# Three edits around the fusion of a convolution block: who requests border, weights and parameters, where the filter kernels and the mixing matrices are computed, and what is left in the last stage before the spectral one

## The chip, the cores and the metric

The kernel runs on 1 core of one Trainium2 chip. The metric is the device time of one execution in microseconds (us). The core has TensorE (PE; its weight loads are PEld), VectorE (DVE), ScalarE (ACT), GpSimd (POOL) and SyncE (SP), which meet only at semaphores. DMAs are requested by SP, ACT or POOL, each in the order of its own program, and are carried out by the core's 16 DMA engines. SBUF is the on-chip memory, PSUM the matmul accumulators, "the DRAM tensors" (table, xn, y_dram, kern_dram, spec_dram, t_dram) are in device memory.

## What is computed

The input is x of shape (2, 128, 64, 64), float32. One block adds a convolution part, then a token-mixing part:

```python
# four branches (kernel 1, 1, 3, 7): offsets and mask by a convolution, bilinear samples, contraction
offset = conv2d(x, off_w, off_b, pad); mask = 2 * sigmoid(conv2d(x, mod_w, mod_b, pad))
sampled = bilinear_sample(x, py, px) * mask                      # x, zero outside the image
y = einsum('bckhw,ock->bohw', sampled, reg_w)
x1..x4 = relu(group_norm(y));  x5 = relu(group_norm(conv2d(mean(x), pool_w)))
out = relu(group_norm(conv2d(concat(x1..x5), fuse_w)))           # "the fusion"

# token mixing on u = layernorm(tokens), over four lengths T, T/2, T/4, T/8 with weights w_i
U_plus, U_minus = FFT convolutions of u with 16 filters phi
out_i = sum_k sigma_k**0.25 * (U_plus @ Mpp[i,k] + U_minus @ Mpm[i,k]) + sum_{lag<3} u_shifted @ Mu[i,lag]
w = one_hot(argmax(s)) - s + s,  s = softmax(log_weights + gumbel)
t = t + sum_i w_i * out_i
```

Of this, three products depend on weights alone: the transforms of the filters phi (kern), the matrices mixed over the four lengths and split in a rounded and a rest part (mh, ml, from M_phi, w and sigma), and the same for the lag matrices (mus, from Mu and w).

## The kernel before

The program is a row of stages with a barrier between any two; within a stage each engine has its own list. The times of the stages in the profiled execution are in the next section.

**stage_normalise** (L61) normalises image 0 over its channels in 8 groups of 512 pixels. ACT loads x (L215). For a group PE turns it (L158), DVE measures and scales it (L185 to L203), PE turns it back (L168) and ACT copies it into xnpad (L229). The result is written four times, shifted by a row or a column, into the table that is sampled later: four requests for each half of a group (L113), the first half by SP, the second by ACT; SP also writes xn (L144). The table has a zero border: 16 small writes of the tile zero (L131, L134), which SP requests ahead of everything else in its list, after that the 4410 KB of wom, the weights of the offset convolution (L137), and only then the table and xn. POOL copies seven shifted windows (L122). After the turn of group 4, PE waits for wom and convolves the first window (L253, 49 taps) before it turns groups 5, 6 and 7. The stage ends when all engines are through, SP last of all with its waits for every write.

**stage_branches** (L260) does everything of the branches. ACT first requests base, the bias (into P) and rowt (L521 to L524); DVE waits for all three (`params`) before its first operation, base + P (L606); only after this come the offsets of tile 0, 1, 2, 3 (L615 to L643), each of which lets PE convolve the next window (L253) and POOL gather the samples of the tile (L501). From then on, 960 steps (16 groups of 512 pixels, 60 taps) follow: POOL requests four gathers, DVE and ACT blend the corners (L537, L663 to L674), PE turns and contracts them (L776, L788).

**stage_fuse** (L855) first works out the group norm. Then 16 groups follow in loops of four (`Fori`). SP loads 2048 KB of y_dram into one of four buffers yin as soon as the group four before it is fused (L923). ACT applies scale, bias and relu in place, 8 operations (L976). PE multiplies the 8 pieces with fw (L948; an f32 matmul is two records in the trace, so a group has 16). ACT copies the sum out (L969: `fu`), DVE measures it (L1019). At the end of each four ACT waits for the group's own sum before it goes on with the next four.

**stage_sum** adds x, **stage_tokens** (L1087) normalises the tokens, keeps them in uT and writes their transforms to spec_dram.

**stage_mixtures** (L1270) loads the weights of the token part: taps_dft and windows (phi), the parameters lw, gb, sigma, mu, and m_phi in four chunks of 2048 KB (mr). DVE and ACT work out the weights w_i (`wi`) and sigma**0.25. PE transforms the filters in 8 pieces (L1443), ACT rounds each (L1358), DVE takes the rest (L1402), SP stores the three parts to kern_dram. For each of 4 chunks DVE mixes m_phi (L1421 to L1427), ACT rounds (L1363), DVE takes the rest (L1432). Among this PE computes the lag products: 16 regions with 12 matmuls each (24 records, L1453) into two accumulators ps_m, which DVE adds to accum (L1412), four regions after each chunk; SP stores accum to t_dram.

**stage_spectral** and **stage_output** follow and are not touched.

Of the kernel before, what the change touches and what calls it, by code (L numbers as in the profile page):

```python
# [5 lines left out]
B, C, H, W = 2, 128, 64, 64  # L6
HW = H * W
# [6 lines left out]
TS = H + 3  # L14
# [12 lines left out]
S = 16  # L27
# [39 lines left out]
def stage_normalise(nc, x, tables, ident, eps6, xpart, xn, w_om, wom, R, ps_shared):  # L67

    ctx = ExitStack()
    with ctx:  # L70
# [17 lines left out]
        border_written = sem("border_written")  # L88
# [26 lines left out]
        @block.gpsimd  # L115
        def _(pool):
            pool.memset(zero[:], 0.0).then_inc(zero_set, 1)
            pool.memset(xnpad[:], 0.0).then_inc(pad_zeroed, 1)
            pool.wait_ge(pad_zeroed, 1)
            pool.wait_ge(xn_copied, 2)  # L120
            for kx in range(7):
                pool.tensor_copy(first_win[:, kx, :, :], xnpad[:, 0:HR, kx:kx + W]).then_inc(first_copied, 1)  # L122
            pool.wait_ge(first_copied, 7)

        @block.sync
        def _(sp):
            sp.wait_ge(zero_set, 1)
            for slot, (dy, dx) in enumerate(((0, 0), (0, 1), (1, 0), (1, 1))):
                part = slice(slot * C, (slot + 1) * C)
                for y0, y1 in ((0, 2 - dy), (TS - 1 - dy, TS)):  # L130
                    sp.dma_start(grid[y0:y1, :, part].rearrange("y x s -> x y s"),  # L131
                                 zero[:, 0:(y1 - y0) * C].rearrange("p (y s) -> p y s", s=C)).then_inc(border_written, 16)
                for x0, x1 in ((0, 2 - dx), (TS - 1 - dx, TS)):
                    sp.dma_start(grid[2 - dy:TS - 1 - dy, x0:x1, part],  # L134
                                 zero[0:TS - 3, 0:(x1 - x0) * C].rearrange("p (x s) -> p x s", s=C))\
                        .then_inc(border_written, 16)
            sp.dma_start(wom[:], w_om).then_inc(wom_loaded, 16)  # L137
# [9 lines left out]
            sp.wait_ge(border_written, 256)  # L147
# [3 lines left out]
        def _(pe):  # L151
# [11 lines left out]
            for i in range(GI):  # L163
# [70 lines left out]
        with nc.Block() as clearing:  # L234
            @clearing.sync
            def _(sp):
                for s in x_loaded + [zero_set, border_written, pad_zeroed, x_turned, var_ready, sd_ready,
# [22 lines left out]
def stage_branches(nc, x, xn, tables, wom, R, ps_shared, base_om, bias_om, row_off, regw, ident, eps6, om_dram, y_dram, ystats, xpart):  # L260

    ctx = ExitStack()
    with ctx:
# [4 lines left out]
        base = sb("base", [128, 3, TAPS])  # L268
        rowt = sb("rowt", [128, NG * 4])
# [3 lines left out]
        P = sb("P", [128, 3, TAPS])  # L273
# [34 lines left out]
        params = sem("om_params")  # L308
# [211 lines left out]
        def _(act):  # L520
            act.dma_start(base[:], base_om).then_inc(params, 16)  # L521
            act.dma_start(P[:], bias_om.rearrange("(a k) t -> a k t", a=1).to_broadcast([128, 3, TAPS]))\
                .then_inc(params, 16)
            act.dma_start(rowt[:], row_off).then_inc(params, 16)  # L524
# [76 lines left out]
        def _(dve):  # L601
# [3 lines left out]
            dve.wait_ge(params, 48)  # L605
# [249 lines left out]
def stage_fuse(nc, gate, y_dram, ystats, xpart, pool_w, fuse_w, gnp, gnf, blk16, blk8, eps5, fu, fa, fb):  # L855

    ctx = ExitStack()
    with ctx:
# [27 lines left out]
        fsd = sb("fsd", [C, B])  # L886
        ps_s = ctx.enter_context(nc.psum_tensor("ps_s", [128, 2, 64], F32))
# [21 lines left out]
        fsd_ready = sem("fsd_ready")  # L909
# [955 lines left out]
```

## Time and profile before

| | us |
|---|---|
| Runs (3): median, lowest, highest | 6398.62, 6391.32, 6402.8 |
| Profiled execution: its own time | 6402.89 |
| Its span, first to last instruction | 6401.2 |
| stage_normalise | 0 to 87 |
| stage_branches | 87 to 4955 |
| stage_fuse | 4956 to 5121 |
| stage_sum, stage_tokens | 5121 to 5239 |
| stage_mixtures | 5239 to 5342 |
| stage_spectral, stage_output | 5342 to 6401 |

Over the span PE is busy 82%, DVE 76%, POOL 61%, ACT 41%. These are averages over stages with different limits. The profile is read by stages: in each, which engine's list or which transfer ends last. Its own time is 1.7 us more than its span. A row of a timeline gives the start in us, the time it covers in us, the engine (SPq and ACTq are requests of DMAs by SP and ACT), the line, the operation, what it writes and reads, how many instructions (x), and in brackets how long the engine was idle before it and what ended that.

### The profile page before, as it was taken

The numbers are of one execution on the slowest core, as the hardware profiler recorded it, in microseconds if no ns is written. First come the engines' busy times: TensorE is split into PE (matmuls) and PEld (weight loads), VectorE is DVE, ScalarE is ACT, GpSimd is POOL, SyncE is SP. The second block draws the span as 40 slices with busy tenths as digits, with TensorE's granted clock in tenths as the row PEclk, the third lists the DMA queues.
The fourth block names the chain that finished last, engine by engine and source line by source line (L and its number), as shares of the span: only waits on it lengthen the run. The fifth ranks groups of instructions, "written<-read, shape, count | busy, mean of one in ns | idle before, by whom it ended". The sixth has DMA issues, their size and how long they took to land. (4 is left out here: it accounts for less than half of the span.)

```text
span 6401.2 us, 66500 instructions
## 1 busy us (share of the span) xinstructions
PE 5219.2 (82%) x16608; PEld 2633.4 (41%) x16608; DVE 4849.9 (76%) x6696; ACT 2640.8 (41%) x6416; POOL 3908.6 (61%) x4370
## 2 busy tenths in 40 slices
PE   4988888788887878888887888876666748999998
PEld 4433333333333333333333333322222326777777
DVE  2888988888788888878788887878777165666664
ACT  0343434343333434333333333333333633666663
POOL 2777777777777777777777777777776002222221
PEclk8999999999999999999999989998887878999999
DMA  6787877777777777777777777777776565555555
GB/s 219 217 243 223 243 230 243 230 223 221 227 228 219 226 224 222 222 226 218 228 216 234 210 233 210 231 212 229 220 213 202 208 236 183 148 148 146 152 152 178
DMA packets 582036, 1359.17 MB, mean 212 GB/s; under 512 B 95452, under 2 KB 262784, under 8 KB 579972
## 3 DMA queue, kind: packets, MB, share of 16 engines
q0 software_dynamic: 327680, 1044.66, 55.9%
q1 hardware_dynamic: 225748, 292.33, 14.2%
q10 hardware_dynamic: 28336, 19.10, 1.0%
q8 instruction: 104, 1.70, 0.1%
q14 instruction: 168, 1.38, 0.1%
HBM read 1240.28 MB, written 115.46 MB: 212 GB/s over the span
## 5 line engine op out<-in xcount | busy, mean ns | idle before, releaser
L501 POOL DMA_INDIRECT G<-table,om x3840 | 3633.4, 946 | 1215.2 <-issue 1154.0
L788 PE MATMUL ps_y<-sT,R 128*128 128x512 f32 x3840 | 2028.1, 656 | 24.0 <-ACT yb L553 23.8
L663 DVE TENSOR_TENSOR G<-G,ps_w 128x1536 f32<-128x1536 f32 x960 | 1681.4, 1751 | 468.2 <-DMA G<-table,om 452.4
L537 ACT ACTIVATE ps_a<-G,om 128x128 f32<-128x128 f32 x3840 | 1192.6, 357 | 1812.8 <-DMA G<-table,om 1130.6
L776 PE MATMUL ps_t<-ident,acc 128*128 128x128 f32 x3840 | 662.2, 298 | 909.1 <-DVE acc L674 890.4
L776 PEld LDWEIGHTS ps_t<-ident,acc 128*128 128x128 f32 x3840 | 433.6, 147 | 1665.9 <-DVE acc L674 1554.6
L545 ACT ACTIVATE sT<-ps_t 128x512 f32<-128x512 f32 x960 | 572.2, 596 | 1109.0 <-PE ps_y L788 1106.7
L788 PEld LDWEIGHTS ps_y<-sT,R 128*128 128x128 f32 x3840 | 722.5, 209 | 593.3 <-issue 590.7
L1580 DVE TENSOR_TENSOR vl<-ps_v,vh 128x512 fp32r<-128x512 f32 x1024 | 656.9, 686 | 335.0 <-ACT vh L1529 335.0
L1514 POOL DMA_DIRECT2D ut<-spec_dram x512 | 262.6, 513 | 895.8 <-PE ps_v L1595 637.8
L667 DVE TENSOR_TENSOR ps_a<-G,ps_a 128x512 f32<-128x512 f32 x960 | 668.5, 696 | 131.0 <-ACT ps_a L537 31.8
L674 DVE TENSOR_TENSOR acc<-G,ps_a 128x512 f32<-128x512 f32 x960 | 659.7, 687 | 103.0 <-DVE ps_a L671 4.1
L758 PE MATMUL ps_c<-xr,wom 128*128 128x512 f32 x1470 | 721.2, 611 | 0.0
L758 PE MATMUL ps_shared<-xr,wom 128*52 128x512 f32 x1470 | 719.4, 609 | 0.0
L1529 ACT ACTIVATE vh<-ps_v 128x512 fp32r<-128x512 f32 x1024 | 580.4, 596 | 297.6 <-PE ps_v L1595 270.9
L671 DVE TENSOR_TENSOR ps_a<-G,ps_a 128x512 f32<-128x512 f32 x960 | 667.1, 695 | 31.8
L758 PEld LDWEIGHTS ps_c<-xr,wom 128*128 128x128 f32 x1470 | 291.8, 200 | 379.7 <-issue 379.7
L1618 PE MATMUL ps_yf<-vh,mh 128*128 128x512 f32 x1024 | 413.6, 404 | 0.0
L1618 PE MATMUL ps_yf<-vh,ml 128*128 128x512 f32 x1024 | 411.2, 402 | 0.0
L1618 PE MATMUL ps_yf<-vl,mh 128*128 128x512 f32 x1024 | 409.2, 400 | 0.0
L1595 PE MATMUL ps_v<-tt,ut 96*128 96x512 f32 x1024 | 367.5, 401 | 16.8 <-DMA ut<-spec_dram 14.9
L758 PEld LDWEIGHTS ps_shared<-xr,wom 128*52 128x52 f32 x1470 | 154.9, 126 | 505.6 <-issue 505.6
(184 smaller groups left out, 2407.6 us busy)
## 6 DMA issues: line engine op xcount, KB each, us to landing
tt<-kern_dram SPq DMA_DIRECT2D x512, 192.0 KB, 3.4
G<-table,om POOLq DMA_INDIRECT x3840, 3.7
y_dram<-yb SPq DMA_DIRECT2D x64, 512.0 KB, 4.7
yin<-y_dram SPq DMA_DIRECT2D x16, 2048.0 KB, 8.3
ut<-spec_dram POOLq DMA_DIRECT2D x256, 96.0 KB, 3.3
spec_dram<-spec_hi SPq DMA_DIRECT2D x64, 256.0 KB, 2.6
ut<-spec_dram POOLq DMA_DIRECT2D x256, 48.0 KB, 3.0
om_dram<-om_next SPq DMA_DIRECT2D x60, 150.0 KB, 3.5
```

Source lines behind the costliest of these rows:

```text
L501: pool.indirect_dma_start(G[k % RING][:, j, :], None, tables[g // GI], bass.IndirectOffsetOnAxis(ap=om[g % 2][:, j, 0, k:k + 1].bitcast(I3 ...
L537: last = nc.scalar.activation(ps_a[:, j, :], G[k % RING][:, j, 0:C], ACT.Copy, scale=om[g % 2][:, j, 1, k:k + 1])
L663: nc.vector.tensor_tensor(three, three, ps_w[:, :, h:h + 1].to_broadcast([128, 12, C]) .rearrange("p (j c) d -> p j c d", j=4), ALU.mult). ...
L667: nc.vector.tensor_tensor(ps_a[:, :, :], corner(1), ps_a[:, :, :], ALU.add).then_inc(added, 1)
L671: nc.vector.tensor_tensor(ps_a[:, :, :], corner(2), ps_a[:, :, :], ALU.add).then_inc(added, 1)
L674: nc.vector.tensor_tensor(acc[n % 3][:, :, :], corner(3), ps_a[:, :, :], ALU.add).then_inc(blended, 1)
L758: last = nc.tensor.matmul(ps_c2 if rest else ps_c[:, :], cols[:, 128:128 + REST] if rest else cols[:, 0:128], rows, start=(tap == 0), stop ...
L776: last = nc.tensor.transpose(ps_t[:, 128 * j:128 * j + 128], acc[n % 3][:, j, :], ident[:, :])
L788: last = nc.tensor.matmul(ps_y[:, half, :], R[:, k, 128 * half:128 * half + 128], sT[n % 2][:, :], start=(k == t0), stop=(k == ends[br] - 1))
L1529: nc.scalar.activation(vh[c][:, n, :, :], spread(ps_v[n % BANKS]), ACT.Copy).then_inc(v_high, 1)
L1580: nc.vector.tensor_tensor(vl[c][:, n, :, :], spread(ps_v[n % BANKS]), vh[c][:, n, :, :].bitcast(F32), ALU.subtract).then_inc(v_low, 1)
L1618: last = nc.tensor.matmul(ps_y[q][:, :], m[:, c, k, :], v[c][:, :, k, :], start=(c == 0 and k == 0 and n == 0), stop=(c == 1 and k == KF - ...
```

## The change

**Start.** The 16 border writes are requested by POOL: the 8 of rows behind its two memsets, the 8 of columns behind its window copies. base, the bias and rowt are requested by SP as its first requests in stage_normalise (their tiles live longer now). wom is requested by ACT behind its 8 loads of x. SP's list begins with these three and goes on with table and xn. PE convolves the first window behind the turns of all eight groups. DVE no longer waits for parameters in stage_branches.

**Fusion.** The loops of four are written out, so that ACT applies relu to group g before it copies out g-1, for all g. Between the groups stands what was in stage_mixtures, apart from the lag products: PE transforms filter piece g-2 behind group g (g = 2 to 9), ACT rounds and DVE subtracts piece g-4, DVE mixes a chunk of m_phi at g = 4, 7, 10, 13, and ACT and DVE split it at g = 6, 9, 12, 15. SP's loads and stores for this stand between its loads of y. mr is one buffer (before: two), kern_hi and kern_lo hold a quarter each of what they held.

**stage_mixtures** holds only the lag products, into four accumulators, the adds and the stores of t_dram.

The core of the diff:

```diff
@@ stage_normalise: POOL, SP, PE, ACT
             pool.wait_ge(pad_zeroed, 1)
+            pool.wait_ge(zero_set, 1)
...
+            for slot in range(4):
+                dy, dx = divmod(slot, 2)
+                zero_rows(slot, 0, 2 - dy)
+                zero_rows(slot, TS - 1 - dy, TS)
             pool.wait_ge(xn_copied, 2)
             for kx in range(7):
                 pool.tensor_copy(first_win[:, kx, :, :], xnpad[:, 0:HR, kx:kx + W]).then_inc(first_copied, 1)
+            for slot in range(4):
+                dy, dx = divmod(slot, 2)
+                zero_columns(slot, dy, 0, 2 - dx)
+                zero_columns(slot, dy, TS - 1 - dx, TS)
             pool.wait_ge(first_copied, 7)
+            pool.wait_ge(border_written, 256)
 
         @block.sync
         def _(sp):
-            sp.wait_ge(zero_set, 1)
-            for slot, (dy, dx) in enumerate(((0, 0), (0, 1), (1, 0), (1, 1))):
...
-            sp.dma_start(wom[:], w_om).then_inc(wom_loaded, 16)
+            sp.dma_start(base[:], base_om).then_inc(params, 16)
+            sp.dma_start(P[:], bias_om.rearrange("(a k) t -> a k t", a=1).to_broadcast([128, 3, TAPS])).then_inc(params, 16)
+            sp.dma_start(rowt[:], row_off).then_inc(params, 16)
...
-                if i == 4:
-                    pe.wait_ge(first_copied, 7)
-                    pe.wait_ge(wom_loaded, 16)
-                    convolve_window(nc, ps_shared, first_win, wom, 0).then_inc(first_done, 1)
+            pe.wait_ge(first_copied, 7)
+            pe.wait_ge(wom_loaded, 16)
+            convolve_window(nc, ps_shared, first_win, wom, 0).then_inc(first_done, 1)
...
                 act.dma_start(xg[i][:, :], x[0, :, i * CH:i * CH + CH]).then_inc(x_loaded[i], 16)
+            act.dma_start(wom[:], w_om).then_inc(wom_loaded, 16)
@@ stage_branches: DVE
             dve.sem_inc(sig_used, 1)
-            dve.wait_ge(params, 48)
@@ stage_fuse
+        mixed_at = {4 + 3 * c: c for c in range(NM)}
+        split_at = {6 + 3 * c: c for c in range(NM)}
...
+            def store_kernel(q):
+                sp.wait_ge(k_low, 2 * q + 2)
...
+            for g in range(YR, NG):
+                load_y(g)
+                if g in (9, 12, 15):
+                    load_m(g // 3 - 2)
+                if g % 2 == 0 and 8 <= g <= 14:
+                    store_kernel(g // 2 - 4)
...
+            def kernel_transform(n):
+                q, c = kernels[n]
+                if n == 0:
+                    pe.wait_ge(phi_loaded, 32)
+                if n >= 2:
+                    pe.wait_ge(k_low, n - 1)
...
+            for g in range(NG):
...
+                last.then_inc(fused, 1)
+                if 2 <= g < 2 + NK:
+                    kernel_transform(g - 2)
...
+                last.then_inc(z_ready, 1)
+                if g:
+                    copy_out(g - 1)
+                if g == 2:
+                    act.wait_ge(z_max_ready, 1)
+                    nc.scalar.activation(ys[:], lw[:], ACT.Exp, bias=sm[:, 1:2]).then_inc(e_ready, 1)
+                    nc.scalar.activation(sg[:], sg[:], ACT.Sqrt).then_inc(sig_rooted, 1)
...
+                if 4 <= g < 4 + NK:
+                    round_kernel(g - 4)
+                if g in split_at:
+                    round_mixed(split_at[g])
+            copy_out(NG - 1)
...
+            for g in range(NG):
+                dve.wait_ge(fu_ready, g + 1 + YR)
+                nc.vector.bn_stats(fstats[:, 6 * g:6 * g + 6], fu[:, g * CH:g * CH + CH]).then_inc(fu_measured, 1)
+                if g == 0:
+                    segment_max()
+                if g == 2:
+                    segment_weights()
+                if 4 <= g < 4 + NK:
+                    split_kernel(g - 4)
+                if g in mixed_at:
+                    mix(mixed_at[g])
+                if g in split_at:
+                    split_mixed(split_at[g])
@@ stage_mixtures
+        ps_m = [ctx.enter_context(nc.psum_tensor(f"ps_m{q}", [C, 4, NB], F32)) for q in range(4)]
...
             for n, (b, p, q) in enumerate(regions):
-                pe.wait_ge(added, n + 1)
+                if n >= 4:
+                    pe.wait_ge(added, n - 3)
```

Two places show how the lists moved. First SP at the head of stage_normalise, before (zero is the border's tile, the branch is the stage's entry, xt a group of image 0):

```order
L125 UNCONDITIONAL_BRANCH
L131 DMA table0<-zero 67x2x128
L131 DMA table0<-zero 67x128
L134 DMA table0<-zero 64x2x128
...
L137 DMA wom<-in_w_om 128x8820
L113 DMA table0<-xt0 64x4x128 x4
L144 DMA xn0<-xnpad 128x770
```

and now:

```order
L146 UNCONDITIONAL_BRANCH
L148 DMA base<-in_base_om 128x180
L149 DMA P<-in_bias_om 128x180
L150 DMA rowt<-in_row_off 128x64
L114 DMA table0<-xt0 64x4x128 x4
L157 DMA xn0<-xnpad 128x770
```

The 16 border writes and wom are gone from the front of SP's list; the table's writes stand behind three small loads.

Second PE in the fusion, with the semaphores that a row waits for. Before, in the loop's body (groups 0 and 1 of the four; a row of REGISTER_ALU counts for the next wait):

```order
L948 MATMUL ps_f0<-yin0,fw 128x512 [waits fu_ready,z_ready]
L948 MATMUL ps_f0<-yin0,fw 128x512 x7
L945 REGISTER_ALU
L948 MATMUL ps_f1<-yin1,fw 128x512 [waits fu_ready,z_ready]
L948 MATMUL ps_f1<-yin1,fw 128x512 x7
```

and now (groups 3 and 4, each followed by a filter piece ps_k):

```order
L1025 MATMUL ps_f3<-yin3,fw 128x512 [waits fu_ready,z_ready]
L1025 MATMUL ps_f3<-yin3,fw 128x512 x7
L1017 MATMUL ps_k1<-windows,taps_dft 128x512
L1025 MATMUL ps_f0<-yin0,fw 128x512 [waits fu_ready,z_ready]
L1025 MATMUL ps_f0<-yin0,fw 128x512 x7
L1017 MATMUL ps_k0<-windows,taps_dft 128x512 [waits k_low]
```

From group 4 to group 9 a filter piece that waits for DVE (`k_low`) stands between two groups on PE. What it waits for is the subtraction in DVE's list, here at group 4, behind the measure of that same group; before, the only DVE row of a group was its measure (L1019):

```order
L1164 BN_STATS fstats<-fu 128x6 [waits fu_ready]
L1142 TENSOR_TENSOR kern_lo<-ps_k,kern_hi 128x512 [waits k_high]
L1149 TENSOR_SCALAR mw<-mr,wi 128x1024 [waits m_loaded]
L1151 SCALAR_TENSOR_TENSOR mw<-mr,wi,mw 128x1024 [waits s_step] x3
L1153 TENSOR_TENSOR mt<-mw 128x512 [waits s_step]
```

The subtraction and the mixing of a chunk have moved from stage_mixtures to behind a measure.

## Rows read from the trace of the kernel before

**Rows 1.** Busy time by stage: us, PE, PEld, DVE, ACT, POOL, granted clock, DMA share, GB/s.
```profile
0.00:87.00 87.00, 30.51 (x162) 26.77 (x162) 26.08 (x112) 7.79 (x17) 10.98 (x15) 0.92 0.72 213
...
4955.00:5121.00 166.00, 124.38 (x268) 54.36 (x268) 20.50 (x65) 103.45 (x147) 0.00 (x0) 0.86 0.59 207
...
5239.00:5342.00 103.00, 72.77 (x400) 59.48 (x400) 50.85 (x87) 14.68 (x29) 0.00 (x0) 0.81 0.51 199
```

**Rows 2.** Timeline of SP's requests in stage_normalise.
```profile
4.59 2.68 SPq L131 DMA_DIRECT2D table<-zero  x2
...
33.95 5.12 SPq L134 DMA_DIRECT2D table<-zero  x2
39.11 0.60 SPq L137 DMA_DIRECT2D wom<-in_w_om  x1
...
76.81 3.97 SPq L113 DMA_DIRECT2D table<-xt  x4
80.82 0.61 SPq L144 DMA_DIRECT2D xn<-xnpad  x1
```

**Rows 3.** Timeline of ACT's requests and of PE in stage_normalise.
```profile
29.42 2.79 ACTq L113 DMA_DIRECT2D table<-xt  x4
...
53.09 15.83 PE L253 MATMUL ps_shared<-wom,R 128*128 128x180 f32 x98 [25.80 <-DMA wom<-in_w_om]
...
73.50 3.65 ACTq L113 DMA_DIRECT2D table<-xt  x4
```

**Rows 4.** The DMA request of wom: count, size, us to landing.
```profile
wom<-in_w_om SPq DMA_DIRECT2D x1, 4410.0 KB, 13.8
```

**Rows 5.** Timeline at the head of stage_branches, DVE and POOL.
```profile
103.23 0.35 DVE L606 TENSOR_TENSOR base<-base,P 128x180 f32<-128x180 f32 x1 [24.36 <-DMA rowt<-in_row_off]
...
108.43 1.16 POOL L501 DMA_INDIRECT G<-table,om  x1 [19.90 <-DVEq L646]
```

**Rows 6.** Costliest groups of the page: the gathers; busy, mean ns, idle before.
```profile
L501 POOL DMA_INDIRECT G<-table,om x3840 | 3633.4, 946 | 1215.2 <-issue 1154.0
```

**Rows 7.** Timeline of the fusion: PE, ACT and DVE at groups 0 to 3.
```profile
4973.77 15.84 PE L948 MATMUL ps_f<-yin,fw 128*128 128x512 f32 x32 [6.65 <-ACT yin L976]
...
4983.41 0.69 ACT L969 ACTIVATE fu<-ps_f,bias 128x512 f32 x1 [4.07 <-PE ps_f L948]
...
4984.00 5.73 ACT L976 ACTIVATE yin<-yin,ybb,ya 128x512 f32<-128x512 f32 x8
...
4984.39 0.69 DVE L1019 BATCH_NORM_STATS2 fstats<-fu  x1 [17.08 <-ACT fu L969]
...
4989.78 14.00 PE L948 MATMUL ps_f<-yin,fw 128*128 128x512 f32 x32 [0.18 <-ACT yin L976]
```

**Rows 8.** Timeline of the fusion: PE from group 4, DVE at the last group.
```profile
5010.51 19.92 PE L948 MATMUL ps_f<-yin,fw 128*128 128x512 f32 x40 [6.72 <-ACT yin L976]
...
5116.57 0.69 DVE L1019 BATCH_NORM_STATS2 fstats<-fu  x1 [6.16 <-ACT fu L969]
```

**Rows 9.** DMA requests of the fusion.
```profile
yin<-y_dram SPq DMA_DIRECT2D x16, 2048.0 KB, 8.3
```

**Rows 10.** DMA requests of stage_mixtures.
```profile
mr<-in_m_phi SPq DMA_DIRECT2D x4, 2048.0 KB, 11.4
```

**Rows 11.** Timeline of stage_mixtures.
```profile
5251.12 1.28 ACT L1352 ACT_TABLE_LOAD   x1 [22.45 <-DVE sm L1374]
...
5261.97 0.69 DVE L1402 TENSOR_TENSOR kern_lo<-ps_k,kern_hi 128x512 fp32r<-128x512 f32 x1 [2.20 <-ACT kern_hi L1358]
...
5267.92 6.77 PE L1453 MATMUL ps_m<-uT,mus 128*128 128x64 f32 x48
...
5270.14 3.92 DVE L1423 SCALAR_TENSOR_TENSOR mw<-mr,wi,mw 128x1024 f32<-128x1024 f32 x3
...
5285.23 1.67 DVE L1432 SCALAR_TENSOR_TENSOR ml<-mt,sigma_b,mh 128x256 fp32r<-128x256 f32 x4
...
5336.96 0.69 DVE L1412 TENSOR_TENSOR accum<-accum,ps_m 128x512 f32<-128x512 f32 x1 [2.62 <-PE ps_m L1453]
```

More of the change, by code:

```diff
@@ L64, in first_window, with stage_normalise @@
     return flat(R[:, WIN_TAP:TAPS, :])[:, 0:7 * HR * W].rearrange("c (k r x) -> c k r x", k=7, r=HR)
-def stage_normalise(nc, x, tables, ident, eps6, xpart, xn, w_om, wom, R, ps_shared):
+def stage_normalise(nc, x, tables, ident, eps6, xpart, xn, w_om, wom, R, ps_shared, border_written,
+                    base_om, bias_om, row_off, base, P, rowt):
     ctx = ExitStack()
@@ L257, in convolve_window, with stage_branches @@
     return last
-def stage_branches(nc, x, xn, tables, wom, R, ps_shared, base_om, bias_om, row_off, regw, ident, eps6, om_dram, y_dram, ystats, xpart):
+def stage_branches(nc, x, xn, tables, wom, R, ps_shared, base, P, rowt, regw, ident, eps6, om_dram, y_dram, ystats, xpart):
     ctx = ExitStack()
@@ L886, in stage_fuse @@
         fsd = sb("fsd", [C, B])
+        lw = sb("lw", [128, SEG])
+        gb = sb("gb", [128, SEG])
+        sm = sb("sm", [128, 4])
+        ys = sb("ys", [128, SEG])
+        wi = sb("wi", [128, SEG])
+        sg = sb("sigma_b", [128, KF])
+        mu = sb("mu", [C, SEG, 3, C])
+        mr = sb("mr", [C, KC, 2, SEG, C])
+        mw = sb("mw", [C, KC, 2, C])
+        mt = sb("mt", [C, 2, KC, C])
+        windows = sb("windows", [NB, 2, 2 * S * KF])
+        taps_dft = sb("taps_dft", [NB, 4, NF])
+        khi = [sb(f"kern_hi{h}", [NF, 2, 2 * S * KF], F32R) for h in range(2)]
+        klo = [sb(f"kern_lo{h}", [NF, 2, 2 * S * KF], F32R) for h in range(2)]
+        ps_k = [ctx.enter_context(nc.psum_tensor(f"ps_k{q}", [NF, CH], F32)) for q in range(2)]
         ps_s = ctx.enter_context(nc.psum_tensor("ps_s", [128, 2, 64], F32))
@@ L1014, in _ @@
             nc.vector.tensor_copy(bias5[:], ps_s[:, 1, 0:B]).then_inc(b5_ready, 1)
[L1015 to L1020 removed]
+            ss = Steps(dve, s_step)
@@ L1021, in _ @@
+            dve.wait_ge(m_split, KF)
             dve.wait_ge(fu_measured, NG)
@@ L1434, in _ @@
-            dve.wait_ge(m_split, KF)
+            for n, (b, p, q) in enumerate(regions):
+                dve.wait_ge(mixed, n + 1)
+                acc = accum[:, 2 * b + p, 4 * q:4 * q + 4, :]
+                nc.vector.tensor_tensor(acc, acc, ps_m[n % 4][:, :, :], ALU.add).then_inc(added, 1)
         @block.tensor
         def _(pe):
-            pe.wait_ge(phi_loaded, 32)
-            for n, (q, c) in enumerate(kernels):
-                if n >= 2:
-                    pe.wait_ge(k_low, n - 1)
-                nc.tensor.matmul(ps_k[n % 2][:, :], taps_dft[:, q, :], windows[:, c, :],
-                                 start=True, stop=True).then_inc(k_done, 1)
@@ L1452, in _ @@
                         s0 = 1 + 4 * q + shift
-                        last = nc.tensor.matmul(ps_m[n % 2][:, :, lo:hi], mus[:, lag, seg, :],
+                        last = nc.tensor.matmul(ps_m[n % 4][:, :, lo:hi], mus[:, lag, seg, :],
                                                 uT[:, 2 * b + src, s0:s0 + 4, lo:hi],
@@ L1765, in program @@
             ps_shared = held.enter_context(nc.psum_tensor("ps_shared", [128, CH], F32))
-            stage_normalise(nc, d["x"], tables, ident, eps6, xpart, xn, d["w_om"], wom, R, ps_shared)
-            stage_branches(nc, d["x"], xn, tables, wom, R, ps_shared, d["base_om"], d["bias_om"], d["row_off"], d["regw"], ident, eps6,
+            base = held.enter_context(nc.sbuf_tensor("base", [128, 3, TAPS], F32))
+            P = held.enter_context(nc.sbuf_tensor("P", [128, 3, TAPS], F32))
+            rowt = held.enter_context(nc.sbuf_tensor("rowt", [128, NG * 4], F32))
+            stage_normalise(nc, d["x"], tables, ident, eps6, xpart, xn, d["w_om"], wom, R, ps_shared, border_written,
+                            d["base_om"], d["bias_om"], d["row_off"], base, P, rowt)
+            stage_branches(nc, d["x"], xn, tables, wom, R, ps_shared, base, P, rowt, d["regw"], ident, eps6,
                            om_dram, y_dram, ystats, xpart)
```

344 lines of the change are left out of this document (143 added, 201 removed).

## The prediction, made before the changed kernel had run

> **What bounds the kernel now.** I read the profile by stages, since no engine bounds the whole span. First the page's group of gathers [rows 6]: 3840 gathers of 946 ns, each with some 0.30 us of POOL's own issue before it (1154 us for all), make 4787 us of the 4868 us of stage_branches. That is 5.0 us for each of the 960 steps, and nothing in the change is in these steps. So this stage keeps its length from its first gather on, and what counts is when that gather starts. Three places are left: the time up to the first gather (108.4 us, [rows 5]), the fusion (166 us) and stage_mixtures (103 us, [rows 1]).
>
> Up to the first gather, SP's list is what ends last. Its border writes run from 4.59 to 39.07, wom is requested at 39.11, and the last write of xn at 80.82 [rows 2]; the stage ends at 87.1. PE idled 25.8 us for wom and then convolved for 15.83 us [rows 3]. In the next stage DVE starts at 103.23 only, released by rowt, a small load that lies behind the large loads of that moment [rows 5]: 16.1 us after the stage's start.
>
> In the fusion PE does a group in 7.0 us at full clock (32 records, two groups, in 14.00) and ACT's relu takes 5.73 us [rows 7]. At the end of each four groups PE waits 6.7 us for ACT, and its next groups begin at the lower clock level: 40 records in 19.92 us [rows 8], where 40 at 14.00/32 take 17.5, so 2.4 us more. From PE's first group to the last group's measure it takes 5116.57 - 4973.77 = 142.8 us [rows 7, 8].
>
> In stage_mixtures DVE and the loads set the pace: PE is busy 72.8 us of 103 and DVE 50.9 [rows 1], yet they alternate. The lag products alone are 6.77 us for two regions [rows 11].
>
> **The start.** (a) Parameters. They are requested 80 us earlier, so DVE's wait of 16.1 us goes. What is next: DVE needs only the first window's sum, which PE has finished before the stage begins. R's load is first needed after three windows. Gain 16 us; I see no row that would take it back.
>
> (b) Border and wom. SP loses 34.5 us at the front of its list (4.59 to 39.07). What is late next has three candidates. First, SP's own remaining list: eight groups of four table writes and one of xn, 3.97 + about 0.7 us each when ACT writes too [rows 2], from 14.3 us on: 52, plus about 5 for landing and barrier. Second, the DMA engines. They are busy 0.72 of 87 us [rows 1] = 62.6 us, and none of this work goes. Started at 4.3 and kept at 0.95 it ends at 70; with 2 us of barrier, 72. Third, ACT and then PE. ACT's table writes lie behind wom in its own queue. Alone it needs 3.3 us a group (2.79 of requests and the rest, [rows 3]), with SP beside it 3.65 (the requests, [rows 3]) + 0.9; eight groups from 14.3 are 40 to 51. wom takes 13.8 us to land [rows 4], and a queue that is full of it holds ACT up by at most about 9 us more. Then PE's convolution, 15.8 us [rows 3], now stands behind the last turn instead of the fifth: its end is 40 + 15.8 = 56 at the earliest, about 57 + 15.8 = 73 at the latest likely, and 2 us of barrier. I take 73 for the end of the stage, since the second and the third candidate both point there: 14 us gained. The ends are 57 (30 us gained) and 87 (nothing gained, if writes of 512 bytes from three queues hinder each other).
>
> The Trainium skill, in "DMA: Bandwidth & Descriptors", section "Issuing engines are not separate DMA queues", says that transfers requested by several engines run on the same 16 DMA engines and interleave, so that spreading requests saves only the time of issuing them. This speaks against part (b). By that rule the 62.6 us of work stay a floor and the stage ends at 72; without it, by the lists alone, at 57 to 59.
>
> POOL's 16 border requests: those of rows lie in POOL's idle time before its copies, those of columns behind them. No row shows such a request on POOL; the nearest are gathers at 1.25 us [rows 6], 20 us in all, from about 9 to 45. That is before 73, so I put nothing. Even at SP's 2.2 us each they would be done at 50.
>
> Start: -14 - 16 = -30 us, ends -16 and -46.
>
> **The fusion.** Removed: the stops of the loops. With relu(g+1) issued before copy-out(g), ACT needs 5.73 + 0.69 = 6.4 us a group, under PE's 6.9, so the wait of 6.7 us and the 2.4 us of lower clock after each four are gone. Added on the path:
> - At group 2 ACT loads two tables (1.28 us each [rows 11]) and does three small operations, about 3.5 us. Relu(3) ends that much later; PE waits about 2.0 us and does its first filter piece, 0.9 us (two records of 14.00/32). Together 2.9. The second piece waits for nothing: 0.9.
> - Pieces 2 to 7, behind groups 4 to 9, wait for DVE. After PE ends a group, ACT starts the copy-out 0.15 us later, DVE's measure starts 0.98 us after it (4983.41 to 4984.39 [rows 7]), the subtraction 0.65 later, and it takes 0.74 to release PE (its 0.69 and the step [rows 11]); then the piece, 0.87. That is 3.4 us between two groups, six times: 20.4. I assume that PE keeps its full clock over a wait of 2.5 us.
> - ACT's splitting at groups 6 and 9 hides in these waits. At group 12 ACT has 5.73 + 0.69 + 1.71 = 8.1 us, 1.1 more than PE.
> - DVE's mixing (3.92 for three of its six operations [rows 11], 6.0 in all) lies behind the subtraction at groups 4, 7, 10, 13, in periods of 10.3 or 7 us: hidden.
>
> Sum: groups 0 and 1 16.0, fourteen groups of 6.9 are 96.6, then 2.9 + 0.9 + 20.4 + 1.1, and 1.1 to the last measure: 139.0, against 142.8. Behind the last measure DVE splits the last chunk, 1.67 us [rows 11], which nothing hides. Fusion: -3.8 + 1.7 = -2 us.
>
> The transfers: 34 MB became about 50 MB. y comes in 8.3 us for 2048 KB [rows 9], mr in 11.4 [rows 10]; the loads of y are requested four groups ahead, two are needed at most at once, and through the slow groups each has 20 us. The tight end is the last: y 15 lies behind the last kern stores, which wait for DVE, and the last mr behind y 15. By these rows it lands about where DVE wants it, 3 us late, with 0.4 us to spare for ACT. Each us later costs one. At wom's rate (4410 KB in 13.8 us [rows 4]) all transfers need 152 us instead of the 147 that are there: +5.
> Ends for the fusion: -6 (two of the six waits shorter) and +17.
>
> **stage_mixtures.** 103 us become: eight times 6.77 = 54.2 us of PE [rows 11], with 2.4 us for a start at the lower level [rows 8], the last add 0.69 at 5336.96 and from its end to the stage's end 4.9 us [rows 11], 0.3 at the start: 62.5. With four accumulators DVE's adds are hidden (0.69 against 3.39 a region). Gain 40 us; ends 37 (3.4 us a region become 3.6) and 42.
>
> **The sum.** -30 - 2 - 40 = -72 us. The profiled execution took 6402.9 us (span 6401.2), so it would take 6331. The median of the three runs is 6398.6, 4 us less: 6326.6. I predict 6327.
>
> **The rivals.**
> 1. The fusion grows (17%). The six waits of 2.5 us let PE's clock fall, each paid with 2.4 us [rows 8]: +14. For it: PE's granted clock is 0.86 over the fusion [rows 1]. Against it: the falls shown come behind waits of 6.7 us. 6341.
> 2. The start gives only the parameters' wait (13%): the DMA engines are slower with mixed writes, the stage still ends near 87. For it: 0.72 of busy share already. 6341.
> 3. The start gives all (17%): the stage ends at 57, when SP's and ACT's lists are through. For it: 0.28 of the engines' time is free, and small writes on one queue are slow by their issue. 6311.
> 4. Slower (3%). PE stays at its lower level through the whole fusion, because filter pieces and waits break its work up. Fourteen groups cost 6.9 us more each, the eight pieces 0.9: +104. With the start and stage_mixtures as forecast: 6398.6 - 70 + 102 = 6431. It decides from about two thirds of the groups at the lower level on.
> 5. The change doesn't do what it says (2%): the work moved into the fusion is paid there in full (DVE and the transfers, 40 us) and the start's gain is lost behind the first gathers: within 0.2% of before.
> Forecast as summed: 48%.
>
> **Range and chances.** 6303 to 6350 holds cases 1 to 3 and the forecast with the ends of their terms (-46 - 6 - 42 = -94 is its far edge, taken as 6305 less the runs' spread). A measurement of this kernel can tell about 0.2% (13 us) from no change. Faster by more than that: 95%; within: 2%; slower: 3%.
>
> **What would show it.** Right: the first stage ends near 73 and the first gather starts near 78; DVE's first operation of stage_branches comes within 1 us of its start; the last gather starts as many us earlier as the first. In the fusion PE waits for DVE's subtraction six times, some 2.5 us each, and no longer for ACT at each fourth group; clock 1.0 after the first groups. stage_mixtures about 62 us, PE without gaps. Wrong: a wait of ACT for y or of DVE for mr near the fusion's end; PE records of 0.86 us spacing in the middle of the fusion; ACT held at its table writes behind wom for more than 10 us; or gathers with a period other than 5.0 us.

## The result and the profile after

| | before | changed |
|---|---|---|
| Median of 5 runs each (lowest, highest), us | 6396.09 (6391.32, 6402.8) | 6363.78 (6359.82, 6364.0) |
| Profiled execution, its span | 6402.89, 6401.2 | 6363.91, 6362.2 |
| stage_normalise ends at | 87.1 | 80.2 |
| first gather, last gather start at | 108.4, 4936.2 | 85.7, 4943.2 |
| stage_fuse | 4956.0 to 5121.4 | 4963.6 to 5125.9 |
| stage_mixtures | 5239.3 to 5342.5 | 5244.1 to 5306.2 |
| rest of the span | 1058.7 | 1056.1 |

The ratio is 0.9944 with a 95% interval of 0.9933 to 0.9955: 0.56% faster, 39 us by the spans where 72 were forecast. 6363.8 lies above the range's end of 6350. In spans: first gather -22.7, the stream of gathers +29.7, what lies between it and the fusion +0.6, fusion -3.1, sum and tokens +0.3, mixtures -41.2, the last stages -2.6.

The rows that answer to those shown of before. The page's groups of gathers, as [rows 6] (busy, mean ns, idle before):

```profile
L510 POOL DMA_INDIRECT G<-table,om x3840 | 3660.3, 953 | 1202.2 <-issue 1157.8
```

953 ns instead of 946. POOL's own issue hardly differs (1157.8 us against 1154.0). Of the one line (name, count, ns of the shortest, median and longest, start of first and last), before and then changed:

```profile
L501 POOL DMA_INDIRECT G<-table,om x3840: 942/946/1158, 108.4 to 4936.2; - x192
```

```profile
L510 POOL DMA_INDIRECT G<-table,om x3840: 947/953/1061, 85.7 to 4943.2; - x192
```

The shortest has grown by 5 ns and the median by 7: nearly every gather is some 7 ns longer, from the first hundreds to the last. 3840 x 7 ns are 27 us, POOL's issue adds 3.8 us, and first to last gather takes 4857.5 us instead of 4827.8.

Busy time by stage, as [rows 1], of the changed kernel:

```profile
0.00:80.20 80.20, 30.53 (x162) 26.62 (x162) 26.51 (x112) 7.78 (x17) 26.55 (x31) 1.00 0.85 234
4963.50:5125.90 162.40, 124.36 (x284) 54.35 (x284) 60.18 (x136) 116.77 (x176) 0.00 (x0) 0.92 0.85 312
5244.00:5306.00 62.00, 56.48 (x384) 53.31 (x384) 11.00 (x16) 0.00 (x0) 0.00 (x0) 0.94 0.17 68
```

In the first stage the DMA engines are 0.85 busy for 80.2 us: 68.2 us of work, where before they had 0.72 x 87 = 62.6. Its timeline (ACT's requests, POOL's, SP's, then PE and the next stage, as [rows 2, 3, 5]):

```profile
9.04 0.46 ACTq L228 DMA_DIRECT2D wom<-in_w_om  x1
...
22.34 11.46 ACTq L114 DMA_DIRECT2D table<-xt  x3
33.85 0.61 ACT L242 ACTIVATE xnpad<-ps_n 128x512 f32<-128x512 f32 x1 [15.52 <-issue]
```

```profile
9.06 11.06 POOL L124 DMA_DIRECT2D table<-zero  x8 [0.31 <-POOL xnpad L119]
...
40.69 4.56 POOL L128 DMA_DIRECT2D table<-zero  x8
...
85.69 1.03 POOL L510 DMA_INDIRECT G<-table,om  x1 [4.04 <-DVEq L650]
```

```profile
19.33 14.99 SPq L114 DMA_DIRECT2D table<-xt  x4
...
73.22 0.61 SPq L157 DMA_DIRECT2D xn<-xnpad  x1
```

```profile
63.04 14.46 PE L266 MATMUL ps_shared<-wom,R 128*128 128x180 f32 x98
```

Both queues are held at group 1's table writes (11.5 and 15 us), ACT's copy of group 1 comes at 33.85, PE's convolution at 63.04 and the stage ends at 80.2. POOL's 8 requests of rows take 11.06 us, 1.38 each in the mean, its 8 of columns 0.57 each. Requests of the border (count, KB, us to landing):

```profile
table<-zero POOLq DMA_DIRECT2D x4, 67.0 KB, 17.0
table<-zero POOLq DMA_DIRECT2D x4, 64.0 KB, 3.6
```

Rows (67 KB, requested at 9 us beside wom) land after 17 us, columns (64 KB, requested at 41 us) after 3.6. In the next stage DVE's first operation comes 0.3 us after the stage's start: the wait of 16 us of [rows 5] is gone.

The fusion, PE, as [rows 7, 8] (one group and one filter piece; six of these waits), and its end:

```profile
5014.84 7.03 PE L1025 MATMUL ps_f<-yin,fw 128*128 128x512 f32 x16
5023.96 1.12 PE L1017 MATMUL ps_k<-windows,taps_dft 128*128 128x512 f32 x2 [2.10 <-DVE kern_lo L1142]
```

```profile
5109.59 0.76 DVE L1149 TENSOR_SCALAR mw<-mr,wi 128x1024 f32<-128x1024 f32 x1 [3.20 <-DMA mr<-in_m_phi]
...
5119.43 0.69 DVE L1164 BATCH_NORM_STATS2 fstats<-fu 128x6 f32<-128x512 f32 x1 [3.19 <-ACT fu L1043]
5120.04 1.65 DVE L1159 SCALAR_TENSOR_TENSOR ml<-mt,sigma_b,mh 128x256 fp32r<-128x256 f32 x4
```

stage_mixtures, as [rows 11]:

```profile
5244.10 56.48 PE L1461 MATMUL ps_m<-uT,mus 128*128 128x64 f32 x384 [12.29 <-PEq L1236]
```

The fusion and stage_mixtures came as forecast; the start gave less, and the gathers took back more than the start gave: the last gather starts 7.0 us later than before, though the first starts 22.7 us earlier.

### The profile page after: what moved, and what is told of

Same layout as the page of the kernel before. It is cut to its first block and busy times, and to the rows that moved or that the text cites. A ratio compares the mean times of both kernels' runs of the same rounds, so it can differ in the third digit from the quotient of the medians.

```text
span 6362.2 us, 66252 instructions
## 1 busy us (share of the span) xinstructions
PE 5196.9 (82%) x16608; PEld 2627.8 (41%) x16608; DVE 4850.7 (76%) x6696; ACT 2639.4 (41%) x6416; POOL 3950.9 (62%) x4386
## 3 DMA queue, kind: packets, MB, share of 16 engines
q14 instruction: 168, 1.38, 0.1%
## 5 line engine op out<-in xcount | busy, mean ns | idle before, releaser
L510 POOL DMA_INDIRECT G<-table,om x3840 | 3660.3, 953 | 1202.2 <-issue 1157.8
```

Of the source, the lines that this page charges most:

```text
L510: pool.indirect_dma_start(G[k % RING][:, j, :], None, tables[g // GI], bass.IndirectOffsetOnAxis(ap=om[g % 2][:, j, 0, k:k + 1].bitcast(I3 ...
```

## The experiments

The kernels are named by what they change. "Stream" is the time from the first gather to the last; the page's ns per gather stands beside it.

| kernel | border by | ns | stream, us | first gather | profiled run, us |
|---|---|---|---|---|---|
| before | SP, 16 | 946 | 4827.8 | 108.4 | 6402.9 |
| changed | POOL, 16 | 953 | 4857.5 | 85.7 | 6363.9 |
| border_sp | SP, 16 | 946 | 4829.2 | 96.2 | 6344.5 |
| fusion_alone | SP, 16 | 946 | 4826.1 | 109.1 | 6356.4 |
| border_pool_alone | POOL, 16 | 953 | 4853.4 | 96.7 | 6413.4 |
| merged_on_pool | POOL, 8 | 953 | 4857.5 | 75.1 | 6353.1 |
| border_merged | SP, 8 | 946 | 4830.7 | 88.4 | 6343.0 |
| merged_by_act | ACT, 8 | 946 | 4828.1 | 90.7 | 6341.8 |
| rows_of_64 | POOL, 8 of 64 | 949 | 4841.0 | 74.9 | 6336.1 |

**1. Which edit makes the gathers longer: border_sp, border_pool_alone, fusion_alone.** border_sp is the changed kernel without this:

```diff
-            for slot in range(4):
-                dy, dx = divmod(slot, 2)
-                zero_rows(slot, 0, 2 - dy)
-                zero_rows(slot, TS - 1 - dy, TS)
...
+            for slot, (dy, dx) in enumerate(((0, 0), (0, 1), (1, 0), (1, 1))):   # sync, behind rowt
```

> The changed kernel with one edit undone: SP requests the 16 border writes again (behind the three parameter loads, ahead of the table), POOL requests nothing before its gathers. The semaphore border_written and the held tiles base, P, rowt stay where the change put them. Theory A (POOL's own 16 plain requests make each later gather longer): the gathers are 946 ns again instead of 953, first to last gather 4828 us instead of 4857.5; the start is some 4 us later than in the changed kernel because SP's list begins with 34 us of border writes again; time about 6364 - 29 + 4 = 6339. Theory B (the tiles that live longer, or the semaphore allocated further out, make the gathers longer): still 953 ns and 4857 us, time about 6368.

border_pool_alone makes the opposite edit in the kernel before:

> The kernel before with one edit: the 16 border writes are requested by POOL (rows behind its memsets, columns behind its window copies), with the semaphore border_written allocated outside the stage. wom stays on SP, now its first request; parameters, fusion and mixtures as before. Theory A (POOL's plain requests make the gathers longer): gathers of 953 ns, first to last 4857 us; the stage's end some 7 to 9 us earlier, DVE's wait for rowt stays; time about 6396 + 30 - 8 = 6418, slower than before. Theory B (held tiles): gathers of 946 ns, about 6388.

fusion_alone has the whole start as before (functions stage_normalise and stage_branches):

> The changed kernel with the whole start undone: stage_normalise and stage_branches as before, only the fusion and stage_mixtures are the changed ones. Both theories A and B: gathers of 946 ns, first gather at 108, fusion and mixtures as in the changed kernel (162 and 62 us, -3 and -41, and 2.6 us in the last stages): 6396 - 47 = 6349, faster than the full change. Rival C (the longer program of the fusion makes the gathers longer): gathers of 953 ns, about 6378.

Measured: border_sp 946 ns, median 6345.57, ratio to before 0.9917 (0.9901 to 0.9934). border_pool_alone 953 ns, 6414.09, 1.0023 (1.0013 to 1.0034). fusion_alone 946 ns, 6356.12, 0.9933 (0.9917 to 0.995).

```profile
L501 POOL DMA_INDIRECT G<-table,om x3840 | 3633.4, 946 | 1200.9 <-issue 1156.9
```

```profile
L509 POOL DMA_INDIRECT G<-table,om x3840 | 3660.3, 953 | 1215.1 <-issue 1158.2
```

(border_sp, then border_pool_alone.) Theory A holds: one edit undone gives the 7 ns back and 19 us of the whole; the same edit alone costs 7 ns in the kernel before and makes it slower, although the first gather starts 11.7 us earlier. B and C fall. fusion_alone has 7.5 us less of span than the full change: its first gather is 23.4 us later and its stream 31.4 us shorter. So by the spans the whole edit of the start made the kernel slower; the intervals of the two ratios overlap, so this loss is not clear of noise.

**2. Why the start gave less: wom_behind_3.**

```diff
-            act.dma_start(wom[:], w_om).then_inc(wom_loaded, 16)
...
                 write_table(act, i, 1)
+                if i == 3:
+                    act.dma_start(wom[:], w_om).then_inc(wom_loaded, 16)
```

> The changed kernel with wom requested by ACT behind its table writes of group 3 instead of ahead of all its table writes. Theory D (ACT's table writes held behind wom for 11.5 and 15 us delay the turns, and PE's convolution behind them ends the stage at 80.2): ACT's writes of group 1 take about 3 us, PE's last turn comes near 52 instead of 62, the stage ends at about 70, time about 6354. Rival E (the DMA engines, 0.85 busy over 80 us = 68 us of work, set the end whatever the order): the stage ends at 76 to 80, time 6360 to 6364. The gathers stay 953 ns by theory A and B.

Measured: median 6365.87, 0.9948 (0.9929 to 0.9968), first gather at 85.3 instead of 85.7. One of its four executions took 13926 us and is not in the ratio; the other three took 6362.66 to 6366.46. ACT's hold of 11.5 us in group 1 is gone, but it comes back at group 5, behind the new place of wom, with 12.5 us:

```profile
45.49 7.60 ACTq L114 DMA_DIRECT2D table<-xt  x1
...
53.12 4.87 ACTq L114 DMA_DIRECT2D table<-xt  x3
```

Two stretches of it, with the columns of [rows 1]:

```profile
40.00:50.00 10.00, 2.23 (x8) 1.43 (x8) 5.46 (x20) 1.48 (x4) 1.54 (x3) 0.50 1.02 326
50.00:60.00 10.00, 0.00 (x0) 0.00 (x0) 1.11 (x4) 0.78 (x2) 0.00 (x0) 0.50 1.02 371
```

The DMA engines are full from 40 to 60 while PE does next to nothing. The time is the one that theory E gave, and moving wom within ACT's list doesn't help. Theory D is not refuted by it, since the edit moved ACT's hold instead of taking it away. The other kernels with wom behind ACT's loads of x show how the two hang together. PE's convolution in border_sp and in merged_on_pool (below):

```profile
43.03 15.08 PE L257 MATMUL ps_shared<-wom,R 128*128 128x180 f32 x98
```

```profile
52.58 14.29 PE L257 MATMUL ps_shared<-wom,R 128*128 128x180 f32 x98
```

With no border request on POOL, ACT's three requests at group 1 take 3.5 us and PE's convolution starts at 43.0; with 8 it is 5.8 and 52.6, with 16 it is 11.5 and 63.0. So POOL's border writes beside wom lengthen ACT's hold, and no run here has the one without the other. In border_sp SP's own list, which has the border again, ends the stage at 90.6.

**3. What of the border writes it is: semaphores, requests, pieces, instructions.** border_on_gathered lets the 16 writes signal the semaphore of gather buffer 0, two_semaphores gives the columns a second new one.

> The changed kernel, all 16 border writes still requested by POOL, but they signal a semaphore that the gathers use anyway (that of buffer 0; the waits of buffer 0 count 256 more). border_written is gone. Theory S (each gather costs more because POOL's queue has one semaphore more to serve): 946 ns again, first to last gather 4828 us, 6364 - 29 = 6335. Theory N (the plain requests themselves, their number or their place in POOL's queue): 953 ns, 6364.

> The changed kernel, but the 8 writes of columns signal a second new semaphore. Theory S: the gathers grow once more, to about 960 ns, first to last gather some 4885 us, about 6391. Theory N: 953 ns, 4857 us, 6364.

Both: 953 ns, streams of 4856.5 and 4855.9, 6363.84 and 6360.76 in one run each. The semaphores are not it.

> Kernel border_sp with one of its 16 border writes (top rows of slot 0) requested by POOL on a semaphore of its own, the other 15 by SP. If the 7 ns come with any plain request of POOL ahead of the gathers (or with the one more semaphore that its queue then signals): 953 ns, first to last gather 4857 us, about 6375 for the whole. If they come with the number of requests or descriptors: 946 ns or little more (7/16 ns more), about 6346.

> Kernel one_on_pool with its one POOL request cut into 16 (the same 134 pieces of 512 bytes, 16 requests). Theory R (the number of plain requests ahead of the gathers shifts something by request): gathers of 953 ns as with 16 border writes, first to last gather 4857 us. Theory P (the number of pieces, 134 against some 1570, counts) or theory I (POOL's instructions) with few of them: 946 ns, 4828 to 4830 us.

```diff
-            pool.dma_start(grid[0:2, :, 0:C]...
+            for i in range(16):
+                x0, x1 = 4 * i, 4 * i + 4 if i < 15 else TS
+                pool.dma_start(grid[0:2, x0:x1, 0:C]...
```

> Kernel border_sp and, on POOL, one additional request of 1536 pieces of 4 bytes (from zero into a tile that nothing reads). Theory P: 953 ns, 4857 us. Theory R: 946 ns, 4828 us, as with one request.

> Kernel border_sp with 48 small memsets on POOL behind its window copies, no DMA added. Theory I (the place of POOL's instructions, shifted by the new ones ahead of the gathers, is what counts): 953 ns. Theories R and P: 946 ns, 4828 us.

All four: 946 ns, streams of 4830.0, 4829.8, 4831.0 and 4830.5, 6343 to 6346 us. Neither a request as such, nor 16 of them, nor one with 1536 pieces (of 4 bytes, into SBUF), nor POOL's other instructions lengthen a gather. Theories R, P (in this form) and I fall.

**4. Rows or columns: rows_on_pool, columns_on_pool, merged_early.**

> Kernel border_sp with the 8 writes of rows requested by POOL at 9 us (on a semaphore of its own) and the 8 of columns by SP. Theory L (what counts is that POOL has requests of columns behind its copies): gathers of 946 ns, 4828 to 4830 us from first to last. Theory K (what counts is whether SP's list has border writes at its front, whoever does the rest): 946 ns. Theory P (the number of pieces that POOL has sent ahead of the gathers, some 800 here): 953 ns, 4857 us.

> Kernel border_sp with the 8 writes of columns requested by POOL behind its copies and the 8 of rows by SP. Theory L: 953 ns, 4857 us. Theory K: 946 ns, 4828 us. Theory P (some 770 pieces): 953 ns.

> Kernel merged_on_pool with all 8 writes requested at 9 us, ahead of POOL's window copies. Theory L (late requests): 946 ns, 4830 us, about 6325. Theories K and P: 953 ns, 4857 us, about 6352.

rows_on_pool 953 ns (stream 4855.4), columns_on_pool 946 ns (4830.0), merged_early 953 ns (4857.6). L, K and P all fall: rows on POOL do it, columns don't, with as many requests (8 each) and nearly as many pieces (804 and 768). Their landings differ too:

```profile
table<-zero POOLq DMA_DIRECT2D x4, 67.0 KB, 17.6
```

```profile
table<-zero POOLq DMA_DIRECT2D x4, 64.0 KB, 2.9
```

(rows_on_pool, columns_on_pool.) But this comes from the moment of the request. The rows are requested at 9 us beside wom, the columns at 33 us. Columns requested at 11 us (merged_early) land late as well, and the rows of wom_behind_3, which has no wom beside them, land after 6.6 us:

```profile
table<-zero POOLq DMA_DIRECT2D x2, 128.0 KB, 14.5
```

```profile
table<-zero POOLq DMA_DIRECT2D x4, 67.0 KB, 6.6
```

Yet the gathers of wom_behind_3 take 954 ns. So a slow landing is not the cause. A row has 67 pieces a side, a column 64. Not tried were rows requested late and columns requested early without rows; the moment alone is not it, since one_on_pool and sixteen_small request at 9 us (946 ns) and columns_of_61 (below) at 33 us (949 ns).

**5. 67 against 64: rows_of_64, columns_of_61.** The base of the first is merged_on_pool (below), that of the second columns_on_pool; what POOL leaves out, SP requests.

```diff
-                pool.dma_start(grid[y, :, s0:s1], zero[:, 0:s1 - s0]).then_inc(border_written, 16)
+                pool.dma_start(grid[y, 0:64, s0:s1], zero[0:64, 0:s1 - s0]).then_inc(border_written, 16)
```

> Kernel merged_on_pool, with POOL's four requests of rows covering 64 of the 67 pieces of a row; SP requests the last three pieces of each (four requests at the front of its list). Theory M (what counts is that POOL's requests ahead of the gathers hold pieces by multiples of 16, as the 64 of a column do and the 67 of a row don't, so that the 16 engines stay level): gathers of 946 ns, first to last gather 4830 us; first gather near 75 as in merged_on_pool, so 6352 - 27 = 6325, the fastest of all. Theory W (rows as such, with their stride, are what counts): 953 ns, 4857 us, about 6352.

> Kernel columns_on_pool (946 ns), with POOL's eight requests of columns covering 61 of 64 pieces each; SP requests the last three of each. Theory M (61 is no multiple of 16): 953 ns, 4857 us, about 6377. Theory W (rows on POOL): 946 ns, 4830 us, about 6350.

Both 949 ns, streams of 4841.0 and 4839.8:

```profile
L506 POOL DMA_INDIRECT G<-table,om x3840: 942/949/1051, 74.9 to 4915.9; - x192
```

```profile
L518 POOL DMA_INDIRECT G<-table,om x3840: 942/949/1062, 100.9 to 4940.7; - x192
```

The crossed pair met in the middle. The 64 pieces took half of the cost off the rows and the 61 put half of it on the columns, so the count of pieces has a part, and neither M nor W holds alone. What 61 does is seen in POOL's requests: the 8 of columns take 10.46 us where 8 of 64 pieces take 4.62 (columns_of_61, columns_on_pool):

```profile
33.30 10.46 POOL L129 DMA_DIRECT2D table<-zero  x8
```

```profile
32.97 4.62 POOL L129 DMA_DIRECT2D table<-zero  x8
```

The Trainium skill, "DMA: Bandwidth & Descriptors", section "Why a DMA increments its semaphore by 16 and not by 1", states that a transfer runs on the largest number of engines up to 16 that divides the slowest dimension of both its sides, that on POOL's queue a transfer on fewer engines takes the next ones in turn, and that on Trainium2 some direct copies from POOL are an exception and are spread over all 16. 67 and 61 are prime, so by the rule such a request lies on one engine. The trace's packets of POOL's queue show both cases. In one_on_pool (one request, two rows of 67) the 67 KB go in 17 packets of up to 4096 bytes, no two of which overlap, from 14.6 to 28.3 us, beside 240 packets of 32 bytes: that agrees with one engine. In rows_on_pool each of the four requests of a single row goes in 13 packets of 5 pieces and one of 2: spread, which agrees with the exception. POOL is busy 2.33 us with the request of one_on_pool and 0.56 us with each single row of merged_on_pool:

```profile
8.77 2.33 POOL L123 DMA_DIRECT2D table<-zero  x1 [0.32 <-POOL xnpad L120]
```

```profile
9.17 2.25 POOL L124 DMA_DIRECT2D table<-zero  x4 [0.31 <-POOL xnpad L119]
```

By that rule POOL's queues on the 16 engines stand unlevel behind requests on one engine. But one_on_pool has one of them at 946 ns, merged_on_pool has none (its rows of 67 are all single) at 953, and rows_of_64, whose data packets are all 4096 bytes long, 12 for each engine if spread evenly, has 949. So neither the rule nor its exception gives the gather's ns, and what inside POOL's requests sets the three levels stays open.

**6. The border in fewer, larger pieces: border_merged, merged_on_pool, merged_by_act.** A row of the border is written for all shifts at once, 8 requests instead of 16:

```diff
+            for y, s0, s1 in ((0, 0, 4 * C), (TS - 1, 0, 4 * C), (1, 0, 2 * C), (TS - 2, 2 * C, 4 * C)):
+                sp.dma_start(grid[y, :, s0:s1], zero[:, 0:s1 - s0]).then_inc(border_written, 16)
+            for x, s, n in ((0, 0, 2 * C), (TS - 1, 0, 2 * C), (1, 0, C), (TS - 2, C, C)):
...
+                sp.dma_start(dst, zero[0:TS - 3, 0:2 * n].rearrange("p (u c) -> p u c", c=n)).then_inc(border_written, 16)
```

> Kernel border_sp (SP requests the border, POOL nothing) with the border in 8 writes instead of 16: a row of the border for all four shifts at once, a column for two or four, in pieces of 512 to 2048 bytes. Same bytes in the same places. If SP's time for the border is a time per request and per piece, it falls from 49 us to about 20 and SP's list ends near 70 instead of 84.5: gathers 946 ns, first gather near 80 instead of 96, about 6345 - 15 = 6330. If the DMA engines set it (0.85 to 1.0 busy already), the first gather comes at 90 to 94 and the time is 6340 to 6344.

> The changed kernel with the border in 8 writes instead of 16 (four of rows, four of columns, as in border_merged), all requested by POOL. If the 7 ns come with 16 requests and not with 8: gathers of 946 ns and a first gather at 85 or a little earlier, 6364 - 29 = 6335 or some us less. If they come with any larger number of requests or pieces (here some 780 pieces): 953 ns, about 6362.

> Kernel border_merged with its 8 border writes requested by ACT at the end of its list instead of by SP at the front; POOL requests nothing before the gathers. Theory K (SP without border writes makes the gathers longer): 953 ns, 4857 us. Theories L and P: 946 ns. The start: ACT's list and SP's list both end near 65 to 70, the first gather comes at 77 to 82 instead of 88.4, so with 946 ns some 6332 for the whole, the fastest so far; with 953 ns 6361.

Medians: border_merged 6340.19, 0.991 (0.9894 to 0.9927); merged_on_pool 6352.18, 0.9929 (0.9912 to 0.9946); merged_by_act 6340.6, 0.9905 (0.9889 to 0.9922). On SP the four rows still held its list for 28.7 us, ahead of the table, so the first gather came at 88.4 and not 80; at ACT's end it came at 90.7. On POOL it came at 75.1:

```profile
0.00:69.60 69.60, 30.35 (x162) 26.43 (x162) 26.55 (x112) 7.77 (x17) 15.80 (x24) 1.00 0.88 270
```

That is 0.88 x 69.6 = 61.2 us of DMA work instead of 68.2, for the same bytes to the same places, and 10.6 us of stage. On SP the 8 are cheaper than the 16 as well: 0.79 x 82.9 = 65.5 us (border_merged) instead of 0.78 x 90.6 = 70.7 (border_sp). Its gathers take 953 ns, so it is behind the others all the same. rows_of_64 has the start of merged_on_pool and 949 ns: median 6337.93, ratio 0.989 (0.9873 to 0.9906), against 0.9944 (0.9933 to 0.9955) for the change. It beats both kernels. From border_merged and merged_by_act it can't be told apart by these intervals.

## Why the prediction was wrong

**The step that failed** is the first: "this stage keeps its length from its first gather on", since "nothing in the change is in these steps". The code of the steps was untouched, yet each of 3840 gathers became 7 ns longer because of requests that POOL had made some 40 to 77 us before the first of them: +29.7 us from the first gather to the last. It was put at 0 with no range, and POOL's requests too ("so I put nothing"), priced by their own time only. The sign "gathers with a period other than 5.0 us" stood among those that would make it wrong, but no rival carried it. The runs show the cause (the border's rows on POOL) and don't show the mechanism.

**The range** was also narrower than its own terms. Its lower end adds up the fast ends of all three terms (-46 - 6 - 42 = -94). The same sum of the slow ends is -16 + 17 - 37 = -36, which from 6398.6 gives 6363, not 6350. The measured 6363.8 lies just there, but that is luck: what was lost was lost in a place that had no term.

**The start** gave 22.7 of 30. The parameters' 16 us came whole. Of the 14 from border and wom 7 came. PE's convolution (to 77.5) and SP's last write of xn (landed at 76.8) end together. The convolution was to begin at about 57 at the latest likely, with ACT held by at most about 9 us behind wom. It began at 63.0: ACT's three requests at group 1 took 11.5 us and the one before them 4.7. By the prediction's own terms the late case was 51 + 9 = 60 already. "ACT held at its table writes behind wom for more than 10 us" came true. The floor of the DMA engines was mis-sized too: it was taken from before as 62.6 us, with "none of this work goes" and none added, and became 68.2. That is not the price of POOL's requests alone, since border_sp, where SP makes them, has 70.7. With the border in larger pieces on POOL it was 61.2, and the stage ended at 69.6, below the 73 forecast. On "Issuing engines are not separate DMA queues": the trace agrees with the rule in that the stage didn't end before its floor, while the lists alone had been put at 57.

**The fusion**: -3.1 for -2. Six waits of PE of 2.1 us, not 2.5, at full clock over each; 138.1 us from PE's first group to the last measure (4981.38 to 5119.43) for 139.0 forecast; 1.65 behind it for 1.67. DVE waited 3.2 us for the last mr as told, and ACT 3.1 us for mt. The groups were summed at 6.9 us where [rows 7] give 7.0 and the trace 7.0; the waits, shorter by 0.4 each, made up for it. Rivals 1 and 4 didn't come: the granted clock over the fusion rose from 0.86 to 0.92 and was 1.00 through the six waits. **stage_mixtures**: 56.5 us of PE where 54.2 + 2.4 stood; -41.2 for -40. fusion_alone, which has these two and the old start, is 43 us below the kernel before (medians 6356.1 and 6399.2 on one chip), where 47 were expected.

**Rivals.** Rival 2 (the start gives only the parameters) was half right on the start; at 6341 it still lacked the 30 us. No case held a loss inside the gathers. Rival 5 spoke of a gain "lost behind the first gathers", by another way and with 2%.

## What to carry to other kernels

A loop whose code a change doesn't touch can still change its pace, if the engine that issues it made other requests earlier (border_sp, border_pool_alone); where a loop has thousands of equal requests, compare the mean ns of one first, since 7 ns were worth more here than all the moves at the start. Price a request that is moved to another queue by what it does to that queue's later requests too, and put its bound into the range. Add up the slow ends of the terms as well as the fast ones. The border was cheaper in 8 requests with pieces of 0.5 to 2 KB than in 16 with pieces of 512 bytes (61.2 against 68.2 us of DMA work on POOL, 65.5 against 70.7 on SP), and it is worth counting the work of the DMA engines of a stage in both kernels (share x length), not only in the one before.

## What was not expected of the hardware

- An indirect gather on POOL takes 946, 949 or 953 ns for the whole stage of 4.83 to 4.86 ms, according to the plain requests that POOL made ahead of it: none, 8 columns of 64 pieces, one request or 16 with 134 pieces in all: 946; 4 rows and 4 columns of 64, 8 columns of 61: 949; 8 rows of 67, with or without columns, also 4 rows of 67 and 4 columns of 64: 953 (954 in wom_behind_3). The cause inside the requests is not known.
- POOL is busy 2.33 us with one request of two rows of 67 pieces (one_on_pool), 0.56 us with one of a single row of 67 (merged_on_pool) and 0.57 us in the mean with one of one or two columns of 64. How long a request takes to land hangs on what else is moving: the same 67 KB took 17.0 us beside wom and 6.6 us without it (wom_behind_3).
- The border's zeros in 16 requests on POOL cost the DMA engines 7 us more than the same zeros in 8 (68.2 against 61.2 us of work in the stage), on SP 5 us more (70.7 against 65.5).
- In wom_behind_3 PE's granted clock was at the lower level (0.50) from 20 to 60 us with PE busy for 7.3 of these 40 us, and the time was still that of the change.
